# State-space layer: the four projections of a group as four one-bank tiles in four consecutive steps, norm and turned h one step forward

## The reference

```python
zxbcdt = einsum('bld,kd->blk', layernorm(x), in_proj_w)      # 256 z, 512 xBC, 32 dt
z, xBC, dt_raw = split(zxbcdt)
conv = sum(xp[:, k:k + L, :] * conv_w[:, k] for k in range(4)) + conv_b   # xp: xBC padded by 3 in front
xBC = silu(conv)                                             # 256 x_ssm, 128 B, 128 C
dt = 0.001 + 0.099 * sigmoid(dt_raw + dt_bias)
Acum = cumsum(dt * A)                                        # per head, 32 heads of 8
y = (C B^T * exp(Acum_q - Acum_s), lower triangle) @ (dt * x_ssm) + D_skip * x_ssm
y = y * silu(z)
y = y * rsqrt(mean(y * y) + 1e-5) * norm_w
out = layernorm(y @ out_proj_w) * ln_w + ln_b
x = x + layernorm(x) + out
```

## Time and profile before

| | us |
|---|---|
| median of 3 runs | 3486.3 |
| lowest, highest | 3482.24, 3488.96 |
| the profiled execution | 3472.24 |
| its span, first to last instruction | 3470.1 |
| mean granted clock of PE | 0.857 of full speed |

### The profile page before, as it was taken

How to read it: one execution, slowest core, us unless ns; L and a number is a source line. 1 busy time by engine, 2 the same in 40 slices (tenths; PEclk the granted TensorE clock), 3 DMA queues, 4 the chain that set the end, 5 groups by cost and what they waited for, 6 DMA issues and landing times. The chain is left out here.

```text
span 3470.1 us, 52901 instructions
## 1 busy us (share of the span) xinstructions
PE 2606.9 (75%) x20619; PEld 1552.8 (45%) x20644; DVE 2095.6 (60%) x4142; ACT 1362.1 (39%) x2355; POOL 580.7 (17%) x581
## 2 busy tenths in 40 slices
PE   5777769999969989987886999688879952344351
PEld 3445436666644434443443444445554531233251
DVE  6888824444458655545655443568773227999757
ACT  4555525555522222222323443257842322444321
POOL 1332400000000023323431000011113021000003
PEclk8888869999979989997988999789979985777675
DMA  1000010000000000001000000020010110000010
GB/s 55 1 2 2 1 33 7 4 4 7 1 4 1 1 30 2 1 2 44 8 8 4 1 1 12 5 87 8 8 46 28 34 41 8 1 0 1 21 55 24
DMA packets 41985, 51.88 MB, mean 15 GB/s; under 512 B 9291, under 2 KB 30868, under 8 KB 40724
## 3 DMA queue, kind: packets, MB, share of 16 engines
q1 hardware_dynamic: 39700, 44.39, 4.1%
q0 software_dynamic: 2048, 4.20, 0.4%
HBM read 39.39 MB, written 9.18 MB: 14 GB/s over the span
## 5 line engine op out<-in xcount | busy, mean ns | idle before, releaser
L130 POOL TENSOR_TENSOR l_rstd<-l_moments,const_minus_half 128x4 f32<-128x4 f32 x104 | 118.1, 1135 | 1621.6 <-DVE l_moments L124 1595.1
L1213 DVE TENSOR_REDUCE l_top<-l_p_score 128x4 f32<-128x1024 f32 x64 | 78.4, 1225 | 223.9 <-PE l_p_score L999 223.9
L1422 PE MATMUL l_p_gate<-l_h_t,w_wg 128*128 128x512 f32 x400 | 209.0, 605 | 0.4 <-issue 0.4
L1445 PE MATMUL l_p_out<-l_hidden,w_wd 128*128 128x512 f32 x400 | 204.4, 594 | 4.2 <-DVE l_hidden L1715 2.9
L2925 DVE SCALAR_TENSOR_TENSOR l_mix<-l_decay,l_cb 128x1024 f32<-128x1024 f32 x128 | 169.3, 1337 | 45.4 <-ACT l_decay L2808 42.9
L796 DVE TENSOR_REDUCE l_top<-l_ring 128x8 f32<-128x1024 f32 x128 | 150.7, 1219 | 67.9 <-PE l_ring L630 67.5
L2808 ACT ACTIVATE l_decay<-l_p_ring 128x1024 f32<-128x1024 f32 x128 | 130.3, 1032 | 148.1 <-PE l_p_ring L2698 146.6
L348 ACT ACTIVATE l_probs<-l_probs,l_minus_top 128x128 f32<-128x128 f32 x512 | 156.8, 393 | 55.7 <-DVE l_minus_top L407 55.6
L1715 DVE TENSOR_TENSOR l_hidden<-l_act_out,l_p_spread 128x512 f32<-128x512 f32 x128 | 85.7, 685 | 129.0 <-ACT l_act_out L1543 128.8
L3185 PE MATMUL l_p_s<-const_ident,l_z 128*128 128x128 f32 x128 | 27.2, 402 | 177.5 <-ACT l_z L3224 177.5
L136 DVE TENSOR_SCALAR l_h<-x_res,l_moments,l_rstd 128x128 f32<-128x128 f32 (+1 forms) x384 | 112.4, 355 | 44.2 <-POOL l_rstd L130 43.9
(11 more groups left out here) (476 smaller groups left out, 6289.5 us busy)
## 6 DMA issues: line engine op xcount, KB each, us to landing
l_c_t<-in_ctx_t SPq DMA_DIRECT2D x24, 256.0 KB, 2.7
l_rows_in<-l_zero SPq DMA_DIRECT2D x1, 2432.0 KB
l_tile_h<-l_rows_in SPq DMA_DIRECT2D x38, 64.0 KB, 1.9
l_rows_out<-l_tile_y SPq DMA_DIRECT2D x38, 64.0 KB, 1.5
w_mask<-in_mask SPq DMA_DIRECT2D x1, 2048.0 KB, 9.2
w_wg<-in_l2f_wg SPq DMA_DIRECT2D x1, 2048.0 KB
w_wu<-in_l2f_wu SPq DMA_DIRECT2D x1, 2048.0 KB
w_wd<-in_l2f_wd SPq DMA_DIRECT2D x1, 2048.0 KB
```

The source lines that it names most:

```text
L130: return nc.gpsimd.tensor_tensor(rstd[:, :], moments[:, :, 1], minus_half[:, 0:moments.shape[1]], ALU.pow)
L1422: nc.tensor.matmul(p_gate[k % 2][:, :], w["wg"][:, s, :], h_t[:, g % 4, :], start=True, stop=True)\
L1445: nc.tensor.matmul(p_out[:, :], w["wd"][:, s, :], hidden[:, k % 4, :], start=(s == 0), stop=(gated and s == steps - 1)).then_inc(down, 1)
```

## The change

The offsets of turned h and of the projections change, and the projections become four tiles that use one bank each of a two-bank buffer. `TURNED` goes from -14 to -15 (n=1), the projections from -12 and -11 (two each) to -13, -12, -11 and -10 (one each, n=3 to 6), `time_steps` from -12 to -13 (n=3), `norm_stats` from -19 to -20 (n=12, now behind `apply_output` of the same step), `norm_apply` from -17 to -18 (n=14, now ahead of `gated(2)`, `copy_products` and `copy_x(k, 0)`). The taps stay where they were. The wait for `y_ready` stays with the first projection.

```diff
-        TURNED, FIRST, SECOND, GATES = -14, -12, -11, -4
+        TURNED, PROJECTED, GATES = -15, (-13, -12, -11, -10), -4
...
-            return sum(NU * k + step < g for k in range(NG) for step in (TURNED, FIRST, SECOND, GATES))
+            return sum(NU * k + step < g for k in range(NG) for step in (TURNED, *PROJECTED, GATES))
...
-                def project(k, pair):
-                    pe.wait_ge(evicted, slot_of(TURNED, k) + 1)
-                    out = ring(slot_of((FIRST, SECOND)[pair], k))
-                    for half in range(2):
-                        c = 2 * pair + half
-                        last = nc.tensor.matmul(out[:, half, :], w["conv_in"][:, c * T:(c + 1) * T], h_t[:, :],
-                                                start=True, stop=True)
-                    last.then_inc(filled, 1)
+                def project(k, c):
+                    if c == 0:
+                        pe.wait_ge(evicted, slot_of(TURNED, k) + 1)
+                    out = ring(slot_of(PROJECTED[c], k))
+                    nc.tensor.matmul(out[:, 0, :], w["conv_in"][:, c * T:(c + 1) * T], h_t[:, :],
+                                     start=True, stop=True).then_inc(filled, 1)
...
-                    if (k := group_at(g + 1, FIRST)) is not None:
-                        project(k, 0)
-                    if (k := group_at(g + 1, SECOND)) is not None:
-                        project(k, 1)
+                    for c in range(NC):
+                        if (k := group_at(g + 1, PROJECTED[c])) is not None:
+                            project(k, c)
...
-                    if (k := group_at(g, -12)) is not None:
+                    if (k := group_at(g, -13)) is not None:
                         time_steps(k)
...
-                def pad_blocks(k, pair):
-
-                    slot = slot_of((FIRST, SECOND)[pair], k)
+                def pad_block(k, c):
+
+                    slot = slot_of(PROJECTED[c], k)
                     act.wait_ge(filled, slot + 1)
-                    if pair == 0 and k >= 2:
+                    if c == 0 and k >= 2:
                         act.wait_ge(y_ready, GROUP * (k - 1))
-                    for half in range(2):
-                        c = 2 * pair + half
-                        source = p_ring[slot % 2][:, half, :].rearrange("p (u t) -> p u t", t=T)
-                        nc.scalar.copy(padded[:, c, :, TAPS - 1:], source)
-                        last = nc.scalar.activation(conv[:, k % 2, c, :, :], source, ACT.Identity, bias=w["conv_b"][:, c:c + 1],
-                                                    scale=w["conv_w"][:, c, TAPS - 1:TAPS])
-                    last.then_inc(evicted, 1)
+                    source = p_ring[slot % 2][:, 0, :].rearrange("p (u t) -> p u t", t=T)
+                    nc.scalar.copy(padded[:, c, :, TAPS - 1:], source)
+                    nc.scalar.activation(conv[:, k % 2, c, :, :], source, ACT.Identity, bias=w["conv_b"][:, c:c + 1],
+                                         scale=w["conv_w"][:, c, TAPS - 1:TAPS]).then_inc(evicted, 1)
...
                     if lag == 0:
-                        dve.wait_ge(evicted, slot_of((FIRST, SECOND)[pair], k) + 1)
+                        dve.wait_ge(evicted, slot_of(PROJECTED[2 * pair + 1], k) + 1)
...
-                    if (k := group_at(g, -19)) is not None:
+                    if (k := group_at(g, -20)) is not None:
                         norm_stats(k)
-                    if (k := group_at(g, -17)) is not None:
+                    if (k := group_at(g, -18)) is not None:
                         norm_apply(k)
-                    if g == -16:
+                    if g == -17:
                         constants()
```

More of the change, by code:

```diff
@@ L2820, in _ @@
                         copy_h(k)
[L2821 to L2824, removed]
+                    for c in range(NC):
+                        if (k := group_at(g, PROJECTED[c])) is not None:
+                            pad_block(k, c)
                     if (k := group_at(g, -8)) is not None:
```

## The result

| | before | after |
|---|---|---|
| median of 5 runs each, us | 3486.3 (3481.9 to 3489.1) | 3464.17 (3457.7 to 3466.9) |
| ratio | | 0.9935, 95% interval 0.992 to 0.9951 |
| profiled execution, its span | 3472.24, 3470.1 | 3457.74, 3455.6 |
| first and last mix of the layer | 37.08, 427.21 | 35.87, 404.70 |

The kernel is 22 us faster; the forecast was 25.6. In the two traces the layer's last mix starts 22.5 us sooner, so the gain is the layer's. The spans of the two profiled executions differ by only 14.5 us: an expert layer with unchanged code took about 17 us more in the one after, and others a few less.

The account below looks back on a forecast made before the run. VectorE was taken as the nearest bound, idle 7.5 us per 51.40 us group. Five groups' 15.0, the first two's 9.8 and the prologue's 0.8 give 25.6 us, from 3486.3 to 3460.7; range 3445 to 3480.

Parts of the forecast that it names:

- prologue: Before the groups: time steps come after two projections, not four; 0.8 us gained after norm_apply's cost of about 0.2.
- first two groups: Groups without GpSimd's output additions and with a longer wait at n=5: 3.9 + 1.0 us each, 9.8 together.
- next five groups: Third to seventh group, with both a projection and GpSimd's output additions: 3.0 us each, 15.0 together.
- what follows them: The last group, which has no projection: nothing gained.
- case A: At n=2, nothing gets between mix and gating; gating ends at 248.85, gain 3.9 us per group.
- case B: At n=2, GpSimd's multiply goes first and delays mix and gating; gating ends at 250.7, gain 2.1 us per group.
- the 5.6 of the forecast: From gating's end to the mix of n=5: eviction, second projection, mixing, time steps, sums tile and decay take 5.6 us.
- the 1.15 us won at n=13 are lost again here: At n=2, transposes of turned h delay the decay, leaving VectorE a 1.1 us gap.
- Rival 2: At the projections, waits go nearly whole, y_ready early and GpSimd out: 37 us gained, 3449; chance 0.20.
- rival 1: Case B with PE's low clock: no gain in five groups, 9 to 10 us in the rest, 3476; chance 0.18.
- rival 3: Filled idle makes GpSimd hold VectorE's mixes or taps 3 to 4 us per group; nothing won, 3484; chance 0.11.
- rival 4: Slower: eviction waits for y_ready, holding the decay of n=4 and second projection; 8 us lost, 3494; chance 0.06.

Follow-up runs that it names:

- norm_only: Kernel before with only norm statistics moved to n=12 and norm_apply to n=14; ratio 0.9923, last mix 402.5 us against 427.2.
- conv_three: The change with three conv buffers instead of two, so the first projection eviction skips the last gating's wait; ratio 0.9899, last mix 391.7 us.
- tiles_later: The change with the four projection tiles one step later, at n=4 to 7, and two conv buffers; ratio 0.9896, last mix 390.3 us.
- tiles_only: The change with norm and turned h back at their old steps, the four one-bank tiles kept; ratio 0.9928, last mix 405.5 us.

## Why the prediction was right, and where it was wrong

| term of the sum | forecast | measured |
|---|---|---|
| prologue | 0.8 | 1.2 |
| first two groups | 9.8 | 12.4 |
| next five groups | 15.0 | 11.8 |
| what follows them | 0 | -2.9 |
| together | 25.6 | 22.5 |

(Measured by the starts of the mixes: the first; n=10 of the second group, 121.54 before and 107.88 after; n=10 of the seventh, 379.02 and 353.56; the last.)

**Right.** VectorE as the bound, idle around the projections; the wait for y_ready with the decay and the second projection behind it, which the trace of before doesn't show; GpSimd's part in it. The five groups show both cases. Where the mix of n=2 began ahead of GpSimd's multiply, the group gained 2.6, 2.7 and 4.5 us (case A: 3.9). Where the multiply was ahead of it, it gained 1.4 and 0.7 (case B: 2.1). The multiply and the mix of n=2 in such a group, from the timeline of after:

```profile
275.31 1.27 POOL L3033 TENSOR_TENSOR l_o<-l_o,w_ln_w 128x512 f32<-128x512 f32 x1
275.44 2.22 DVE L2918 SCALAR_TENSOR_TENSOR l_mix<-l_decay,l_cb 128x1024 f32<-128x1024 f32 x1 [0.36 <-ACT l_decay L2802]
```

**The mis-sized term.** The mean of the five groups was 2.4 us and not 3.0. Four of them came out 0.8 to 1.4 us below their case's number, and these are the four with PE's low clock between n=3 and n=6; the fifth kept the full clock and gained 0.6 more than its case. The prediction priced the low clock at 2.2 us and kept it out of its middle, because PE's wait for own_ready would become shorter. It did, but PE's wait for the buffer ahead of the second projection came in its place (2.4 to 2.6 us). From the end of gating to the mix of n=5 it was 5.8 us in the group with the full clock and 7.3 in the one shown above, for the 5.6 of the forecast (whose own terms give 5.4).

**Wrong.** The step "the 1.15 us won at n=13 are lost again here" failed, and with it the division of the gain. The new wait at n=2 was 0 to 0.6 us, not 1.1. The prediction gave norm and turned h nothing and the tiles everything; the runs give norm alone 24.7 us, and the tiles on top of norm and turned h -4.5. What the step missed: norm_apply stood right ahead of the run of mixes, and with it gone GpSimd's own pair ended 1.3 us sooner; and the old first pair of projections, which it left at the low clock, ran at the full one. The prediction had the own pair done early too, but by a gap at n=2, which norm_only doesn't have, and it didn't follow that the old pairs of projections would then come sooner by themselves: mixing, the sums tile and the first pair all stand behind own_ready on PE. That the total came out near was in part luck: the two parts remove the same idle at n=4 to 6, the first two groups gave 2.6 us more than forecast, and the last group lost 2.9.

**Signs.** The prediction would be wrong by its own words if VectorE's wait at n=5 stayed above 3 us or its busy time per group rose above 45.5. The wait was 2.7 to 2.9 us in four groups and 1.34 in one (1.5 to 2.5 had been expected); the busy time was 44.8 to 45.6, over the mark in one of the five.

**Not foreseen.** What follows the seventh group took 2.9 us more than before. The mean_squares of the last group ran at the low clock (3.58 us for 16 matmuls against 2.17 before), and VectorE waited 4.2 us for it instead of 2.8; the rest are 0.7 us more of waits for decays and a wait of 0.7 for PE's output product. No part of the change touches these; in conv_three and tiles_later, too, the same 16 matmuls took 1.95 us.

**Rival 2**, the waits going nearly whole, is what conv_three and tiles_later do: 35.5 and 36.9 us less than before, near that rival's sum of 37. Between the forecast and it stood the wait for y_ready, for the greater part by the low clock behind it. Rivals 1, 3 and 4 didn't come about whole; of rival 1 the low clock did, in two groups together with case B, and these still gained 0.7 and 1.4 us. Of rival 3 the runs show that its mechanism is real (VectorE's busy time per group rose from 43.90 us to 44.8 to 46.2) at a quarter to two thirds of its 3 to 4 us.

## What to carry to other kernels

When a step is moved forward, look up on every engine what its first instruction waits for, a buffer's last reader above all: a wait that was met over 4 us early (248.84 against 253.32 in the earlier trace rows) is not seen in a trace, and here it cost 13 of 36 us. Price each part of a change also without the others: two parts that remove the same idle don't add, and the second may only cost. Ask of every new wait of PE whether the clock is low behind it: here the change's groups took 47.1 us with the full clock at the projections and 48.5 to 50.6 with the low one. Where two engines hold each other up, as VectorE and GpSimd do here, the length of an instruction of one depends on how the other's instructions stand, also ahead of it; a step can gain by leaving a place, not only by reaching one.

## What the runs showed of the hardware

Three VectorE mixes in a row, each with two operands in SBUF, let two GpSimd instructions in one by one (pair 2.66 us) or not at all until the run had ended (3.95), with the first of GpSimd's instructions shown as started 0.16 us after the first mix in both cases. Four tensor_scalar instructions with scalars from a tile just ahead switched it from the one to the other in every group; one with constants did not. Four with constants gave both outcomes in one execution, and a third between them (3.80 to 3.84).

In the change PE's granted clock was low between n=3 and n=6 in the four steady groups in which PE had waited 2.4 to 2.6 us for a buffer, and full in the one in which it had waited 1.3; after 1.84 us in tiles_only it was the one or the other. At the low clock a projection took 2.08 us and not 1.12, and the stretch from n=3 to n=6 12.5 us and not 9.7 with GpSimd's own pair at 3.95 us in both. Four useless VectorE instructions per group left this clock full in all five steady groups and the layer 10 us shorter in its trace: at this level a gain of 0.3% can come from where instructions fall, not from what is changed.
